# Attention scores of both head lots issued together over four row groups, transposed probabilities in two other PSUM banks

## What is computed

```python
x = x + _L0_xattn_ref(_layernorm(x, axis=-1), ctx_1024, Wq, Wkv, Wout)
# _L0_xattn_ref:
qp = q @ Wq
kp, vp = split(kv @ Wkv)
dots = jnp.einsum('bhid,bhjd->bhij', qh, kh) * scale      # 16 heads of 16
attn = jax.nn.softmax(dots, axis=-1)
out = jnp.einsum('bhij,bhjd->bhid', attn, vh)
return out @ Wout
```

## Time and profile before

| | |
|---|---|
| median of 3 runs | 757.43 us (755.12 to 757.6) |
| profiled execution, own time | 756.54 us |
| its span, first to last instruction | 754.8 us |
| attention 1, first scores to last residual addition | 22.5 to 192.2 us of the span |
| steps 1 to 13, start to start | 9.93 to 10.19 us |
| mean granted TensorE clock | 0.952 |

### The profile page before, as it was taken

How to read it: one execution, slowest core, us unless ns; L and a number is a source line. 1 busy time by engine, 2 the same in 40 slices (tenths; PEclk the granted TensorE clock), 3 DMA queues, 4 the chain that set the end, 5 groups by cost and what they waited for, 6 DMA issues and landing times.

```text
span 754.8 us, 17035 instructions
## 1 busy us (share of the span) xinstructions
PE 657.7 (87%) x4890; PEld 464.8 (62%) x4890; DVE 500.0 (66%) x1180; ACT 375.3 (50%) x878; POOL 291.9 (39%) x358
## 2 busy tenths in 40 slices
PE   2799999997777776898099999999999999999992
PEld 2588888886534545786056666666666666666661
DVE  6389899998588967797954746555464747554430
ACT  1366666665686643786223535363543635543320
POOL 3111111121153625577233736464553637543321
PEclk9799999999999999699589999999999999999996
DMA  8200000000300005336405253533415264421114
GB/s 282 47 15 14 14 14 14 14 0 1 112 0 1 0 1 172 128 82 226 135 23 174 49 150 76 150 85 84 140 31 153 73 181 126 116 43 29 31 15 125
DMA packets 47414, 59.01 MB, mean 78 GB/s; under 512 B 13328, under 2 KB 41168, under 8 KB 47056
## 3 DMA queue, kind: packets, MB, share of 16 engines
q1 hardware_dynamic: 39808, 47.72, 19.5%
q0 software_dynamic: 7536, 10.44, 7.8%
HBM read 145.96 MB, written 11.73 MB: 209 GB/s over the span
## 4 chain that ended last, share of the span: by engine, by line
PE 58%; DVE 20%; issue 8%; ACT 5%; DMA 2%; POOL 2%; DVEq 2%; ACTq 1%; SPq 0%; POOLq 0%
PE psum L1052 19%; PE psum L1074 11%; PE psum L752 5%; PE psum L1065 4%; PE psum L736 3%; PE psum L759 3%; PE psum L772 2%; ACT region L1346 2%; PE psum L791 1%; PE psum L741 1%; PE psum L714 1%; DVE region L1759 1%; DVE region L1777 1%; PE psum L779 1%; DVE region L1956 1%
## 5 line engine op out<-in xcount | busy, mean ns | idle before, releaser
L1052 PE MATMUL psum<-region 128*128 (+1 forms) x936 | 214.8, 379 | 1.6 <-DVE region L1952 1.6
L1052 PEld LDWEIGHTS psum<-region 128*128 128x128 bf16 x936 | 91.5, 98 | 95.5 <-DVE region L1952 1.2
L1329 ACT ACTIVATE region<-psum 128x512 f32<-128x512 f32 x78 | 46.5, 597 | 179.6 <-PE psum L1052 178.7
L675 POOL DMA_INDIRECT sum_dram<-region,row_token x39 | 75.2, 1927 | 135.3 <-DVE region L1948 135.3
L1074 PE MATMUL psum<-region 128*128 (+1 forms) x936 | 110.5, 275 | 5.3 <-DVE region L1956 5.3
L1074 PEld LDWEIGHTS psum<-region 128*128 128x128 bf16 x936 | 91.4, 99 | 18.9 <-issue 7.5
L1931 DVE TENSOR_TENSOR region<-psum,region 128x512 f32<-128x512 f32 x78 | 53.8, 690 | 68.3 <-ACT region L1329 68.3
L545 POOL TENSOR_TENSOR region<-region,pair_mask 128x256 f32<-128x256 f32 x32 | 21.3, 687 | 128.3 <-ACT region L1114 128.3
L1956 DVE TENSOR_TENSOR region<-psum,region 128x1024 bf16<-128x1024 f32 x39 | 47.6, 1221 | 17.7 <-ACT region L1337 17.5
L667 POOL DMA_INDIRECT region<-xrow_dram,row_token x39 | 41.4, 1062 | 38.0 <-DVE row_token L1917 13.6
L1421 DVE TENSOR_REDUCE region<-psum 128x8 f32<-128x1024 f32 x32 | 39.0, 1218 | 18.4 <-PE psum L752 18.4
(11 more groups left out here) (298 smaller groups left out, 1220.3 us busy)
## 6 DMA issues: line engine op xcount, KB each, us to landing
region<-in_L_ffn_w SPq DMA_DIRECT2D x117, 1024.0 KB
region<-in_ctx SPq DMA_DIRECT2D x32, 128.0 KB, 2.4
xrow_dram<-region SPq DMA_DIRECT2D x1, 2080.0 KB, 7.8
x_sb<-in_x SPq DMA_DIRECT2D x4, 512.0 KB, 8.0
region<-in_ctx SPq DMA_DIRECT2D x2, 1024.0 KB, 7.0
region<-neg_max_dram SPq DMA_DIRECT2D x1, 2048.0 KB, 11.5
sum_dram<-x_sb SPq DMA_DIRECT2D x1, 2048.0 KB, 7.5
region<-neg_max_dram SPq DMA_DIRECT2D x4, 256.0 KB, 4.0
```

The source lines that it names most:

```text
L675: pool.indirect_dma_start(sum_dram, bass.IndirectOffsetOnAxis(ap=row_token[:, t:t + 1], axis=0), y_d[:, t % 2, :], None, compute_op=ALU.ad ...
L1052: last = mm(psum[:, 2 * f + n, :], (xT_lo if xl else xT_hi)[:, p, k, :], weights_at(place, wl, n, k * F1 + f * FH, FH), start=(i == 0), st ...
L1329: act_fn(sil_d[:, f, :], psum[:, 2 * f, :], ACT.Silu).then_inc(sil_d_ready, 1)
```

## The change

Three things. Both lots of scores are issued together, once per step, interleaved so that four row groups writing four banks follow each other. The transposed probabilities of both lots go to one buffer of two banks, `PT_ps`, which are banks 0 and 1 of the front; so the transposes of lot 1 wait until ACT has copied those of lot 0, those of lot 0 wait for the copy of the front's projections, and the front transposes wait for the copies of the batch before. The scores wait for DVE's subtractions in place of ACT's copies. And in the statistics after the residual addition, `bn_aggr` writes its result where it is wanted, without a copy.

```diff
+        PT_ps = bank(0, HT, P, count=2)
 # front_transposes
+                if inner or b >= 2:
+                    pe.wait_ge(pt_evac, 2 * (b - 1))
-            def scores(b, p, s, inner=False):
+            def scores(b, p, inner=False):
                 pe.wait_ge(kbd_ready, 2 * b + 2)
                 if inner or b >= 1:
-                    pe.wait_ge(pt_evac, 2 * (b - 1) + s + 1)
+                    pe.wait_ge(shifted_ready, 2 * b)
                 for m in range(KT):
-                    for r in range(2):
-                        rows = slice(32 * (2 * s + r), 32 * (2 * s + r) + 32)
-                        last = mm(S_ps[s][:, 4 * r + 2 * m:4 * r + 2 * m + 2, :], qkT[rows, p, m, :], kbd[rows, p, m, :, :],
-                                  start=True, stop=True)
-                last.then_inc(s_done, 1)
-            def probs_transposes(b, m):
+                    for s in range(2):
+                        for r in range(2):
+                            rows = slice(32 * (2 * s + r), 32 * (2 * s + r) + 32)
+                            last = mm(S_ps[s][:, 4 * r + 2 * m:4 * r + 2 * m + 2, :], qkT[rows, p, m, :], kbd[rows, p, m, :, :],
+                                      start=True, stop=True)
+                        if m == KT - 1:
+                            last.then_inc(s_done, 1)
+            def probs_transposes(b, m, inner=False):
+                if m == 1:
+                    pe.wait_ge(pt_evac, 2 * b + 1)
+                else:
+                    if inner or b >= 1:
+                        pe.wait_ge(pt_evac, 2 * b)
+                    if inner or b + 1 < B:
+                        pe.wait_ge(qk_evac, b + 2)
                 pe.wait_ge(probs_ready, 2 * b + m + 1)
                 for h in range(HT):
-                    last = tr(S_ps[m][:, h, :], probs[:, m, h, :], ident[:])
+                    last = tr(PT_ps[:, h, :], probs[:, m, h, :], ident[:])
                 last.then_inc(pt_done, 1)
 # step on PE
-                scores(b, p, 0, inner)
+                scores(b, p, inner)
 ...
-                scores(b, p, 1, inner)
 ...
 # probsT_copy on ACT
-                act_fn(probsT[:, m, :, :], S_ps[m][:, :, :], ACT.Copy).then_inc(pt_evac, 1)
+                act_fn(probsT[:, m, :, :], PT_ps[:, :, :], ACT.Copy).then_inc(pt_evac, 1)
 # token_stats on DVE
-                nc.vector.bn_aggr(mv1[:], stats[:, 0, :]).then_inc(chain, 1)
+                nc.vector.bn_aggr(mv[:, b, :], stats[:, 0, :]).then_inc(chain, 1)
                 dve.wait_ge(chain, n + 2)
-                nc.vector.tensor_copy(mv[:, b, :], mv1[:]).then_inc(chain, 1)
```

More of the change, by code:

```diff
@@ L806, in step @@
                     tail_b(b - 1)
-                probs_transposes(b, 0)
+                probs_transposes(b, 0, inner)
                 if inner or b >= 1:
                     tail_c(b - 1)
-                probs_transposes(b, 1)
+                probs_transposes(b, 1, inner)
                 values(b, p, 0, inner)
@@ L1440, in tail_add @@
                 dve.wait_ge(x1_ready, b + 1)
-                token_stats(b, ln2_chain, 3 * b)
+                token_stats(b, ln2_chain, 2 * b)
                 for n, op in enumerate((ALU.max, ALU.min)):
@@ L1521, in x1_eps @@
                 part = THIRDS[n]
-                dve.wait_ge(ln2_chain, 3 * part.stop)
+                dve.wait_ge(ln2_chain, 2 * part.stop)
                 nc.vector.tensor_scalar_add(rstd[:, part], mv[:, part, 1], LN_EPS).then_inc(ln2_eps, 1)
@@ L1563, in _ @@
             tail_add(B - 1)
-            dve.wait_ge(ln2_chain, 3 * B)
+            dve.wait_ge(ln2_chain, 2 * B)
             x1_eps(2)
```

## The result

The changed kernel takes 768.26 us (median of 4 runs, 765.25 to 768.59) against 757.51 us: the ratio is 1.0138 with a 95% interval of 1.0104 to 1.0172, slower by 1.4%. Run again later beside other kernels it gave 1.0128 (1.0099 to 1.0156). Forecast: 771, range 767 to 778. The profiled execution took 768.59 us (span 766.7), 12.05 above that of before.

A forecast was written before the change was run, and what follows sets the result against it. The prediction took the ring of releases, not PE's stream, as the bound. Terms 13.03 + 0.17 + 0.99 - 0.07 = +14.1 us on 756.54 gave 770.7, up to 771.6 by the median; forecast 771 us, range 767 to 778.

The forecast's parts named there:

- the ring: Chain of releases from scores through DVE, ACT's copy and values to the next scores; 10.00 us, the whole step.
- Price of the exposed block: Lot 1's transposes, no longer beside ACT's copy, add 0.87 + 0.15 = 1.02 us a step; bounds 0.87 and 1.18.
- Scores together: Issuing both lots of scores at once frees some 1.06 us of PE, but changes lot 0's readiness by 0.
- Only two groups at once: Rival: only two row groups run together, lot 0's maximum up to 0.53 us later a step; 774 to 778, chance 0.10.
- transposes start where the values start today, at 9.36: Lot 1's transposes wait for lot 0's copy and start 9.36 us after the scores, values behind them.
- just fits: PE's instruction stream, busy 9.99 us of a 10.00 us step, was said to only just fit beside the ring.
- DVE takes lot 1 in a queue that has no hole; gain 0: Earlier lot 1 scores, tail and front gain 0, since DVE takes lot 1 only after tail_norm.
- Steps 1 to 13: 13 x 1.02 = 13.26 us, less 0.23 that step 7 already waits for DVE: +13.03 us.
- Step 14: Values waited for DVE's residual addition, starting 10.21 us from the scores; now 10.38, so +0.17 us.
- Step 15: Last step: transposes begin after copy 0 instead of beside it; output copy at 187.61 instead of 186.62, +0.99 us.
- Step 0: First step: projections up to 1.1 us earlier, set against the 1.02 us of exposed transposes; taken as 0.
- The half-clock rival: PE's idling drops the clock to 1.2 GHz, +6.6 us per such step; 778 to 785, chance 0.07.

The follow-up runs named there:

- c_split: Changed kernel with lot 0's transposes in lot 0's own score banks and only lot 1's in the front's banks; ratio to the kernel before 0.9998, 754.72 us.
- g_halves: Changed kernel with ACT's copy of lot 0's transposes split in two halves of one bank each; ratio to the kernel before 1.0044, 759.38 us.
- a_apart: Changed kernel with the scores issued lot by lot in their old places, tail_a behind the second lot; ratio to the kernel before 1.0186, 769.29 us.
- after_again: The changed kernel run once more, unaltered; ratio to the kernel before 1.0128, 766.63 us.
- f_stats: The kernel before with only the statistics edit, bn_aggr writing directly without a copy; ratio to the kernel before 1.0009, 757.16 us.
- e_warm: Changed kernel with matmuls that compute nothing used added in PE's gaps of step 15; ratio to the kernel before 1.0095, 763.66 us.
- b_own: Changed kernel with both lots of transposes back in their own score banks, scores waiting for both copies; ratio to the kernel before 1.0090, 763.48 us.
- i_lotwise: Changed kernel with scores at the same place in PE's order, but lot 0 whole before lot 1; ratio to the kernel before 1.0108, 765.97 us.

## Why the prediction was right, point by point

**The mechanism** held: the ring is the bound, and the shared buffer puts the second transposes on it. Undoing that alone (c_split) returns the step to 9.87, halving the wait (g_halves) returns 0.39 of it, and taking PE's freed 1.06 us away again (a_apart) costs 0.14.

**Price of the exposed block.** 0.87 + 0.15 = 1.02 was taken; 1.03 measured (107.10 to 108.13). That the 0.15 comes from the change of shape was not tested by itself.

**"Scores together" at 0** was right: maximum 1.20 us after the scores, 1.18 before. Only two groups at once, the rival, is refuted by the 16 weight loads in 0.77 us. By the Trainium skill (TensorE: Matmul & The Clock Gate, section Measured speedup vs the span model) I had estimated a round 1.3 times as long; here 16 matmuls take 1.11 us of PE where 8 took 1.07, so no such loss shows.

**The term that was mis-sized is the step length:** +1.02 forecast for a full step, +0.70 measured. The step that failed is where the second transposes start, and with it the belief that PE had nothing else to do before 94.26. Three readings of the earlier trace rows account for most of the difference.

First, "transposes start where the values start today, at 9.36". They start 9.07 after the scores, 0.29 earlier. Between the copy's start and the next PE block lie 1.05 us in the changed kernel and 1.23 before, 0.18 apart. The copies end at 107.05 and 94.07, and in the changed kernel PE starts 0.05 us after the copy's end, not 0.19. Before, the values also stood behind the transposes of lot 1, which had started at 93.19 and need 1.02: 94.21. The waiting was labelled as ACT's, but PE's own queue was the later of the two; c_split's 1.02, with the copy done 0.22 us before, shows the same. PE's stream and the ring were both at their limit, which I had called "just fits".

Second, "DVE takes lot 1 in a queue that has no hole; gain 0". From the maximum of lot 0 to that of lot 1 it is 3.35 us, 3.44 before. The rows of before:

```profile
88.19 0.66 PE L779 MATMUL psum<-ident,region 128*128 128x128 f32 x4
...
88.48 0.40 DVE L1398 TENSOR_SCALAR region<-x_sb,mv,rstd 128x256 f32<-128x256 f32 x1
...
88.88 0.26 DVE L1430 RECIPROCAL region<-psum 128x16 f32<-128x16 f32 x1
...
89.52 1.21 DVE L1421 TENSOR_REDUCE region<-psum 128x8 f32<-128x1024 f32 x1
```

tail_norm (1430) starts 0.40 us after the normalisation did, when tail_a (779, to 88.85) has ended; in the changed kernel it starts 0.32 us after it. It had waited a little for tail_a, hidden under the normalisation.

Third, maximum of lot 1 to exponential is 2.50 instead of 2.56.

These are 0.18 + 0.09 + 0.06 = 0.33; maximum and copy each start 0.02 later, which leaves the 0.29. The next scores follow the values after 0.57 us in place of 0.64, which was not foreseen either, so step 7 has 10.67. a_apart puts tail_a back behind lot 1's scores and returns 0.14 of the 0.09 + 0.06 = 0.15; the two distances are 3.44 and 2.56 there again.

**The other terms.** Steps 1 to 13: +9.05 measured (score start to score start) against +13.03. Step 14: -0.48 against +0.17, because the residual addition that I held fixed came earlier too (181.83, 9.06 after the scores; before 9.67). Step 15 to the last residual addition: +0.99 forecast, +0.8 without the half clock (after_again), +3.0 in the profiled execution with it. Step 0: 0 forecast, -0.58 measured, in a stretch where the clock changes. Start of the first scores: -0.64, not forecast, and of the size by which profiles differ anyway (21.84 here, 21.82 in f_stats, 22.60 in e_warm). Sum of the profile to the last residual addition: -0.64 - 0.58 + 9.05 - 0.48 + 3.02 = +10.37. Past it another 1.5 us came, in stages that the change does not touch and in which the half-clock slices lie elsewhere; what of it is clock was not separated. After_again's span is 6.2 us shorter than the changed kernel's with the same steps. So the forecast of 771 was near the measured 768 for partly cancelling reasons: 4 us too much in the steps, clock time that was not in the sum. The nearness of the total is in part luck.

**The statistics:** forecast 0.07, nothing measurable (f_stats).

**The half-clock rival** did not occur in steps 1 to 14: the clock is 1.00 in step 7, with PE waiting over 1 us in one piece, and 1.00 over all of 33.94 to 183.10. PE was idle for 1.3 us of step 7, not the 2 I had put down. In step 15 half clock did come in the profiled execution, and cost some 2.2 us; that PE's waiting brings it is not shown.

**The rule of the Trainium skill** that speaks against the change (TensorEngine Tiling (Array Packing), section Performance Considerations: packing speeds up TensorE but not the emptying of PSUM) agrees with the changed kernel and with b_own: in both, the use of the packed scores ended at an ACT copy (107.05, 97.24). It does not say which buffer makes the copy hurt; c_split does away with the wait at the same copy time, and then the values wait for PE's own transposes.

## What to carry to other kernels

Follow the ring of releases around a loop before pricing a shorter instruction stream: 1.06 us taken off the busiest engine were worth 0.14 a step, while one wait on a buffer that two users share in turn put a block of 1.03 us on the ring and cost 0.84 a step (a_apart against before). If two blocks of work alternate with their copies, give them different banks, so that the second is written while the first is read; and once the ring is shorter, price the freed engine time anew, since the same packing was then worth 0.54 a step in the profiles. Where a wait's label names an engine that had been done for 0.1 to 0.2 us, look for a second queue that was just as late.

## What was unexpected of the hardware

Matmuls of row groups 2 and 3 issued behind all of those of groups 0 and 1 ran beside them: 16 matmuls of 374 ns (median) in 1.16 us, issued lot by lot, against 1.15 when interleaved (i_lotwise). The same program had 7 us of half clock at 193 us in one profile and none in another, worth 2.2 us there.
